# First sequences of attention between two MoE layers: direct rows loaded ahead of q rows, f projected between a group's last two tiles, -|f| ahead of the norm, and a narrower wait for the first scores

## The reference

```
x = x + 0.5 * moe(norm(x))
x = x + attention(norm(x))
x = x + 0.5 * moe(norm(x))
```

## Time and profile before

| what | value |
|---|---|
| median of 3 runs | 469.72 us (466.66 to 469.98) |
| the profiled execution, its own time | 468.03 us |
| its span in the trace | 465.9 us |
| mean granted clock of TensorE | 0.978 |
| busy: PE / DVE / ACT / POOL | 404.1 us (87%) / 362.4 (78%) / 278.5 (60%) / 249.7 (54%) |

### The profile page before, as it was taken

How to read it: one execution, slowest core, us unless ns; L and a number is a source line. 1 busy time by engine, 2 the same in 40 slices (tenths; PEclk the granted TensorE clock), 3 DMA queues, 4 the chain that set the end, 5 groups by cost and what they waited for, 6 DMA issues and landing times.

```text
span 465.9 us, 11688 instructions
## 1 busy us (share of the span) xinstructions
PE 404.1 (87%) x3280; PEld 287.6 (62%) x3296; DVE 362.4 (78%) x1284; ACT 278.5 (60%) x758; POOL 249.7 (54%) x431
## 2 busy tenths in 40 slices
PE   0778888775799999999999999999998898888884
PEld 0656666553466666666667666766765676666652
DVE  3989999986877786686677678677666458999995
ACT  4666777352275566657566566655656567667753
POOL 8976666543245544544554454454445435676654
PEclk9999999887999999999999999999999899999998
DMA  3311000035644354344535535443540000001001
GB/s 112 92 56 22 0 1 0 1 100 148 171 118 152 117 155 116 111 139 111 149 102 147 134 102 149 113 147 108 152 130 9 6 1 1 25 24 45 23 23 45
DMA packets 45792, 39.11 MB, mean 84 GB/s; under 512 B 5896, under 2 KB 42524, under 8 KB 45754
## 3 DMA queue, kind: packets, MB, share of 16 engines
q1 hardware_dynamic: 43706, 38.14, 29.0%
q10 hardware_dynamic: 2048, 0.53, 0.6%
HBM read 22.61 MB, written 15.20 MB: 81 GB/s over the span
## 4 chain that ended last, share of the span: by engine, by line
PE 43%; POOL 22%; issue 14%; ACT 8%; DVE 5%; DMA 2%; ACTq 2%; SPq 2%; POOLq 1%; DVEq 0%
PE bank L916 10%; POOL m_pair L217 9%; PE bank L901 8%; PE bank L886 6%; ACT a_weights L733 5%; POOL m_upper L221 4%; PE bank L889 4%; PE bank L881 4%; POOL m_rstd L229 3%; PE bank L997 2%; PE bank L1008 2%; ACTq L725 2%; PE bank L1011 2%; DVE a_neg_max L794 1%; DMA x_all<-in_L_attn_x 1%
## 5 line engine op out<-in xcount | busy, mean ns | idle before, releaser
L794 DVE TENSOR_REDUCE a_neg_max<-bank 128x2 f32<-128x512 f32 (+1 forms) x192 | 123.7, 685 | 62.6 <-PE bank L889 59.9
L673 POOL TENSOR_SCALAR_AFFINE_SELECT a_weights<-a_weights 128x512 f32<-128x512 f32 (+1 forms) x96 | 75.5, 787 | 108.7 <-ACT a_weights L733 104.0
L733 ACT ACTIVATE a_weights<-bank 128x512 f32<-128x512 f32 x192 | 107.0, 591 | 35.0 <-issue 22.0
L251 ACT ACTIVATE m_scaled<-bank,m_gates 128x128 f32<-128x128 f32 x256 | 72.3, 365 | 26.2 <-PE bank L417 26.2
L901 PE MATMUL bank<-a_q_rows,a_k_rows 106*128 106x512 f32 (+1 forms) x192 | 73.7, 451 | 4.9 <-ACT a_weights L733 4.9
L217 POOL TENSOR_TENSOR m_pair<-m_scaled 128x256 f32<-128x256 f32 x64 | 47.5, 742 | 50.8 <-ACT m_scaled L251 50.7
L294 DVE SCALAR_TENSOR_TENSOR m_lower<-bank,m_gates,m_lower 128x128 f32<-128x128 f32 x192 | 66.0, 344 | 2.3 <-issue 0.2
L886 PE MATMUL bank<-a_k_rows,a_q_rows 104*128 104x256 f32 x256 | 59.3, 335 | 0.4 <-DVE a_neg_max L794 0.4
L889 PE MATMUL bank<-a_mask,a_ident 128*128 128x256 bf16 (+1 forms) x176 | 56.2, 320 | 0.0
L916 PE MATMUL bank<-a_weights,a_v 128*32 128x128 f32 x1536 | 52.7, 279 | 0.0
L886 PEld LDWEIGHTS bank<-a_k_rows,a_q_rows 104*128 104x128 f32 x256 | 40.6, 194 | 14.5 <-DVE a_neg_max L794 10.1
(11 more groups left out here) (128 smaller groups left out, 828.5 us busy)
## 6 DMA issues: line engine op xcount, KB each, us to landing
a_k_rows<-k_stage SPq DMA_DIRECT2D x16, 416.0 KB
k_stage<-a_k_parts SPq DMA_DIRECT2D x48, 128.0 KB, 1.8
q_stage<-a_q_parts SPq DMA_DIRECT2D x48, 128.0 KB, 1.9
a_q_rows<-q_stage SPq DMA_DIRECT2D x64, 96.0 KB
a_k_heads<-k_stage SPq DMA_DIRECT2D x64, 52.0 KB
a_q_dense<-q_stage SPq DMA_DIRECT2D x16, 192.0 KB
x_all<-in_L_attn_x SPq DMA_DIRECT2D x8, 256.0 KB, 2.8
out_x<-x_all SPq DMA_DIRECT2D x8, 256.0 KB, 2.3
```

The lines of the kernel that those rows point to most:

```text
L251: last = nc.scalar.activation(scaled[:, q % 2, j], y_high[q % 2][:, j * D:(j + 1) * D], ACT.Copy, scale=gates[:, s % 2, q, 4 + j:5 + j])
L673: nc.gpsimd.affine_select(out=diagonal, in_=diagonal, compare_op=ALU.is_ge, fill=0.0, base=0, pattern=[[0, heads.stop - heads.start], [1, P]],
L733: nc.scalar.activation(weights[n // 2][:, half:half + 4, :].rearrange("p h n -> p (h n)"), wt_bank[n % 2][:, :], ACT.Exp).then_inc(wt_exp, 1)
L794: nc.vector.tensor_reduce(neg_max[:, t, heads], score_bank[p % 2][:, :].rearrange("p (h n) -> p h n", n=(t + 1) * P), AX.X, ALU.max, negat ...
```

## The change

Five edits. (1) The string for both early steps becomes `amamamamaa`: attention's part 3 (statistics of s + 3, f on PE) stands between the MoE's tiles 2 and 3 instead of after both. (2) ACT copies f out in part f_part(s) and no longer one part later when s < 0. (3) On DVE -|f| is written ahead of xn; this changes the order only where both fall into the same part, j = 4, for s < 0. (4) SP, for s = -1, loads the direct rows first, then q rows and k rows; for s >= 0 the order stays. In both cases the k_heads loads are now preceded by waits for the stores of k and c. (5) PE's first scores wait until DVE's m_lower chain has 4 x 31 links done and ACT has scaled 31 tiles, instead of for all 32 tiles finished and scaled. The waits for rows_in and direct_in stay.

```diff
--- before.py
+++ after.py
@@ -60,8 +60,8 @@
                 moe(i_moe, i_moe, done)
 
     moe_steps(moe1, -2, groups - 2, after)
-    beside("amamammaaa", -2, moe1, groups - 2)
-    beside("amamammaaa", -1, moe1, groups - 1)
+    beside("amamamamaa", -2, moe1, groups - 2)
+    beside("amamamamaa", -1, moe1, groups - 1)
     run_steps(eng, lambda i, s: [attention(i, s, k) for k in range(6)], 0, seqs - 1, (2, 2 + (seqs - 5) // 3 * 3), 3)
     beside("amaamamaam", seqs - 1, moe2, -2)
     beside("amaamamaam", seqs, moe2, -1)
@@ -460,7 +460,7 @@
         return part
 
     return dict(load_group=load_group, store=store, gpsimd=gpsimd, scalar=scalar, vector=vector, tensor=tensor,
-                tiles_done=upper_used, high_used=high_used)
+                tiles_done=upper_used, high_used=high_used, low_chain=low_chain)
 
 
 def attention_layer(nc, ctx, c, made, banks, x_all, S_LEN, before):
@@ -589,6 +589,18 @@
                     wait_apart(sp, scores_ready, i * 12 + 1, sp_waited)
                 at_least(sp, wt_ready, (i - 1) * 12)
                 sp.wait_ge(q_stored, n * 16 * 3)
+
+                def load_direct():
+                    sp.dma_start(raw(q_dense)[0:NG * 3 * HD, :, :],
+                                 q_dram[b, :, :, :, 0:P].rearrange("r g u n -> (r g) u n")).then_inc(direct_in, 16)
+                    sp.wait_ge(k_stored, n * 16 * 3)
+                    sp.wait_ge(c_stored, n * 16 * 2)
+                    for g in range(NG):
+                        sp.dma_start(raw(k_heads)[g:KR:NG, NU * g:NU * (g + 1), :],
+                                     k_dram[b, :, g, :, 0:P]).then_inc(direct_in, 16)
+
+                if s < 0:
+                    load_direct()
                 for g in range(NG):
                     sp.dma_start(raw(q_rows[b])[g:NG * 3 * HD:NG, NU * g:NU * (g + 1), :],
                                  q_dram[b, :, g]).then_inc(rows_in, 16)
@@ -597,11 +609,7 @@
                 sp.dma_start(raw(k_rows[b])[0:KR, :, :], k_dram[b].rearrange("r g u n -> (r g) u n")).then_inc(rows_in, 16)
                 if 0 <= s:
                     sp.wait_ge(scores_ready, i * 12 + 4)
-                sp.dma_start(raw(q_dense)[0:NG * 3 * HD, :, :],
-                             q_dram[b, :, :, :, 0:P].rearrange("r g u n -> (r g) u n")).then_inc(direct_in, 16)
-                for g in range(NG):
-                    sp.dma_start(raw(k_heads)[g:KR:NG, NU * g:NU * (g + 1), :],
-                                 k_dram[b, :, g, :, 0:P]).then_inc(direct_in, 16)
+                    load_direct()
             if 0 <= s + 2 < NSEQ:
                 b, n = (s + 2) % 3, i + 3
                 sp.wait_ge(qk_lo_done, n * 2)
@@ -750,7 +758,7 @@
                                      ACT.Copy).then_inc(v_copied, 1)
             if j == 3 and S:
                 copy_max(i, s, 0)
-            if j == f_part(s) + 1 and F:
+            if j == f_part(s) + (1 if s >= 0 else 0) and F:
                 act.wait_ge(f_ready, n)
                 nc.scalar.activation(f[:, :], proj_bank[0:H, 0:N], ACT.Copy).then_inc(f_copied, 1)
             if j == f_part(s) + 2 and F:
@@ -840,13 +848,13 @@
                 if s <= 0:
                     dve.wait_ge(before["tiles_done"], 2 * (s + 4) if s < 0 else 2 * NSEQ)
                 statistics(i + 3, n + 1)
-            if j == 4 and 0 <= s + 3 < NSEQ:
-                wait_apart(dve, xt_ready, n, dve_waited)
-                normalised(i + 3, n + 1)
             if j == f_part(s) + 1 and F:
                 dve.wait_ge(f_copied, n)
                 nc.vector.scalar_tensor_tensor(out=neg_abs[:, :], in0=f[:, :], scalar=-1.0, in1=f[:, :],
                                                op0=ALU.mult, op1=ALU.min).then_inc(neg_abs_done, 1)
+            if j == 4 and 0 <= s + 3 < NSEQ:
+                wait_apart(dve, xt_ready, n, dve_waited)
+                normalised(i + 3, n + 1)
             if j == 3 and T:
                 normalise(i - 2, s - 2, 1)
             if j == f_part(s) + 2 and F:
@@ -938,8 +946,8 @@
             if s == 0 and j == 0:
                 pe.wait_ge(set_up, 2)
                 pe.wait_ge(ones_in, 16 * 3 * (NG + 3))
-                pe.wait_ge(before["tiles_done"], 2 * NSEQ)
-                pe.wait_ge(before["high_used"], 2 * NSEQ)
+                pe.wait_ge(before["low_chain"], 4 * (2 * NSEQ - 1))
+                pe.wait_ge(before["high_used"], 2 * NSEQ - 1)
 
             if j == 0 and S:
                 pe.wait_ge(rows_in, (i + 1) * 16 * LOADS)
```

## The result

| | median us (lowest to highest), 12 runs each | ratio to before (95%) |
|---|---|---|
| before, beside it | 466.97 (465.03 to 469.98) | |
| after, first set | 470.44 (467.30 to 473.02) | 1.0064 (1.0035 to 1.0092) |
| after, second set, another session | 467.76 (465.27 to 472.53), before 467.22 | 1.0003 (0.9969 to 1.0038) |

The first set is slower by 0.64%, beyond its interval. The second set of the same kernel shows nothing. Both sets together have a mean of 469.19 us (24 runs); before, over the three sessions of the experiments, has 467.77 (104 runs): the change costs some 1.4 us (0.4 to 2.4 by the spread of the runs), under the 1% that I had called measurable, and of the other sign than my -0.12. One execution of before and one of e12, both of 2020 us, are left out of every mean and ratio here. The profiled execution took 470.74 us (span 468.6) where before took 468.03 (465.9).

A forecast was written before the change was run, and what follows sets the result against it. The attention loop was taken as PE-bound (15.98 of 16.59 us), the first score as waiting on DVE's low parts, SP's issues and the last load. Reorder +0.70 and schedule -0.82 gave -0.12: median 469.72 becomes 469.6 us, range 466.0 to 472.0.

The forecast's parts named there:

- my -0.12: First score at the seam before attention: net shift forecast, +0.70 for the reorder less 0.82 for the schedule, in us.
- The reorder, +0.70: Sequence 0's loads: k rows (416 KB) become last, landing 3.55 us after issue, so the first score comes 0.70 us later.
- the one built on the q rows tile: Upper bound for the k rows' landing: 4.4 us for 96 KB plus 1.2 for the rest, 5.6 us; +3.3 in all.
- late k rows: Rival at the last load: k rows queue behind q rows, land 5.5 us after issue; +1.8, so 471.5 us; chance 0.17.
- The schedule, -0.82: DVE before sequence 0's xn: the wait for rstd disappears, low parts done 0.82 us sooner; ends 0.4 and 1.4.
- The waits, 0: PE's first scores: the relaxed wait, met 4.1 us early and hidden by the loads, is worth 0.
- The clock rival: PE's first scores, 111.2 to 117.6 us: less time at 1.2 GHz, -1.6, so 468.0 us; chance 0.13.
- marks set in advance: Signs expected in the profile after: low parts, load order, last issue, first score and releaser, sequence 1's stores and score, loop pace.

The follow-up runs named there:

- e12: Before with only the narrower wait of the first scores: 469.04 us, ratio 1.0019 (0.9982 to 1.0056).
- e2: Before with only the schedule edits (f between the last two tiles, earlier copy of f, -|f| ahead of the norm): 466.37 us, ratio 0.9998.
- e3: After with the old load order put back, so schedule edits and narrower wait: 465.28 us, ratio 0.9955 to before.
- e11: e3 with -|f| moved back behind the norm: 466.16 us, ratio 0.9965 to before.
- e1: Before with only the new load order for the first sequence (direct rows first, then q rows and k rows): 468.78 us, ratio 1.0031.
- e4: After unchanged, the second set with a second profile: 467.76 us, ratio 1.0003 to before.
- e7: After, with SP waiting for sequence 0's rows to land before issuing sequence 1's stores: 467.87 us, ratio 1.0013 to before.
- e9: After with 16 matmuls whose output nobody reads, in PE's idle time ahead of the first score: 466.12 us, ratio 0.9955 to before.
- e6: After with q rows loaded behind k rows for the first sequence, so a q rows load is last: 466.79 us, ratio 0.9978 to before.
- e5: After, with sequence 0's first scores awaiting only the direct rows, and the other rows two parts later: 466.19 us, ratio 0.999 to before.
- e10: e3 with 10 matmuls whose output nobody reads in the idle time ahead of the first score: 465.03 us, ratio 0.9943 to before.

## Why the prediction was wrong

**The reorder, +0.70: this term was mis-sized, and most of all by its landing.** From the first load issue to the first score the old order takes 9.53 to 10.44 us (before, e12, e2, e3, e11: 10.44, 10.21, 9.81, 9.53, 10.29; mean 10.1), the new one 11.60 to 13.06 (after, e1, e4, e7, e9: 12.31, 11.77, 13.06, 11.84, 11.60; mean 12.1). It costs **2.1 us** (12.12 less 10.06). I drew a line between whole loads of 256 and 512 KB and took 3.55; the k rows landed in 4.15 to 4.70. Those rows are of the inputs, loaded at the start of the kernel; the k rows are gathered from the stage and go behind nine other loads. Which of these differences makes them later no run separates. Of the bounds, the one built on the q rows tile pointed to the right side, and it was put aside for a row "nearest in size". The other half of the error is on the side removed: the last k heads load was taken at its one row of 3.31, and landed in 2.40 to 3.31, 2.93 in the mean of five. The issue times were right: the last issue 7.37 us behind the first (8.20 in e4, by its late c rows), forecast 7.35 and 0.1 for c, where before had 6.99. So the 2.1 is 0.4 of issue (with 0.1 of waiting for c in it; e4 waited 0.8 more), 4.43 (mean of four) less 2.93 = 1.5 of landing, and 0.1 that PE starts 0.24 and not 0.14 us behind it.

**The rival "late k rows"** had this mechanism, deciding from 3.7 us, at a chance of 0.17. My reason against it, that no queue builds up, did not keep the k rows from landing late: 4.15 us even with the stores 2.6 us behind. Whether a queue did build up is not shown. Its size for the landing, 5.5, was too large. I had noted that sequence 1's stores start sooner and priced their meeting with the k rows at nothing: it is 0 to 0.4 us.

**The schedule, -0.82: the mechanism was right.** The 0.82 us of waiting is gone in every profile with the new schedule. The low parts are done there at 94.2 to 96.0, and at 95.07 to 96.56 in the three without; much of this scatter lies ahead of all edits, in when DVE makes sequence 0's xn (84.19 to 85.97). Counted from there they take 10.0 to 10.6 us in ten of the eleven profiles with the new schedule (11.0 in e6), and 10.8, 10.8 and 11.85 without. e1 and e2, with the granted clock at 1.00 there, differ by 0.7; before and e3, at 0.79, by 1.3. So 0.7 to 1.3, within the bounds 0.4 to 1.4. That the subtraction parts from the GpSimd addition, an end of my range, isn't shown: it takes 0.39 us after and 0.74 before, but 0.25 and 0.27 in e1 and e12 with the old schedule.

**The waits, 0: right.** e12 shows it, and e5 why the relaxed wait and the direct rows can't pay as they stand: the first score awaits the rows as well. That this was the limit is only half true, though; without it the next limit is DVE's order, and a third of the gain remains.

**The clock rival came in part, and was taken back.** I gave 0.13 to a shorter stretch at the low level, while naming in its disfavour that PE's idle time in front grows. It did, from 4.4 to 7.95 and 8.82 us, because both halves add to it: the tiles finish sooner and the loads land later. Even so the first step got shorter, from 14.09 to 13.23 and 13.51 us (1.6 were forecast by the rival), and from 111 to 118 us the granted clock was 0.53 before and 0.70 after (0.56 in e4). But a second low stretch followed, 0.72 over 125 to 131 us in both profiles of after where before had 1.00. From the first score to sequence 3's it takes 46.30 and 45.61 us after, 45.60 before: the clock there costs 0 to 0.7 us. The length of the idle time does not order these: e4 with 8.82 us has 45.61, e1 with 5.81 has 46.17, e3 with 5.30 has 45.64.

What e9 says of it: it keeps the new load order and fills the idle time, and the mean falls to 466.17 at a mean clock of 0.9857. That filling it pays in the kernel after is what the runs show; that the idle time is what the change lost by is not shown, and how the 3.0 us divide is not either. In the profiles, e9's first score came 0.92 us later than after's and its sequence 3 0.27 us sooner (156.91 against 157.18, and 157.67 in e4), so the first seam gives 0.3 to 0.8 us in absolute time. But e9's profile was already 1.6 to 1.7 us late at sequence 0's xn, ahead of all edits. Counted from there it gains 1.9 us against after and 2.5 against e4: 0.7 and 2.0 before the first score, where its loads came sooner, which the matmuls don't explain, and 1.2 and 0.5 between the first score and sequence 3's, which can be the clock. In e10 against e3 that last stretch is 0.3 us longer. Another 3.6 us lie at the second seam against the one profile of after, and nothing (30.06 against 30.05) against e4. Why idle time at 103 us should bear on a seam at 350 no run here shows, and it may not.

**What of the 1.4 us is accounted for.** Reorder +2.1 and schedule -0.7 to -1.3 leave +0.8 to +1.4 at the first score. Counted from sequence 0's xn, the first score comes after 26.54 and 27.83 us in the two profiles of after (26.12 in e7, 25.83 in e9) and after 26.50 and 25.23 in those of before and e12, +0.7 in the means. At sequence 3's first score +0.4 (after) and +0.9 (e4) are there in absolute time, against before's 156.81. So about half of the 1.4 or more is what the mis-sized load leaves, and the rest is of the size of the clock's changes at both seams. The fit at equal clock would put all of it down to the clock, but the same fit has e1 1.1 us above before and e3 2.2 below after, which is the order's cost again; the fit can't separate a stall from the clock in it and behind it. The share of each stays open.

The median of the first set, 470.44, lies inside the range of 466.0 to 472.0, and even within 1 us of 469.6. That is luck: the three runs of before that I started from have a median of 469.72, 2.75 us above that of its twelve; beside those the change stands at +3.5 in this set and +0.5 in the second, and not at -0.12. Of the marks set in advance, the new order, the release by k rows, sequence 1's first score some 14 us behind the first (13.23) released by DVE, and the pace (16.5) came true; the last issue at 105.94 came 1.5 us sooner than the 107.4 named, the first score at 110.88 close to 111.1, by two errors that cancel: low parts 1.3 us sooner than the 95.7 named, and a landing 1.15 us later than 3.55. Sequence 1's stores came at 106.44 and not at 108.5: they follow the last load issue at once, as I had said, but I had not moved them by my own -0.82, and that issue was sooner still.

## What to carry to other kernels

Where a consumer waits for a count of all loads, only the last one matters: price a reordering by the landing of the transfer that becomes last, taken from loads issued in the same burst, and by what is released to follow it on the same queue. Work that ends sooner in front of a load that does not only lengthens TensorE's idle time; what the clock then takes was 0 to 0.7 us here, and the length of the idle time did not foretell it. And when a kernel's own runs spread by 5 us, compare the mean granted clock beside the time, look in which stretches it differs and whether the engine had work there, and repeat a set before believing 0.6%.

## What the runs showed of the hardware

- The last load of this burst of ten landed later than loads of more bytes at the start of the kernel: 416 KB in 4.15 to 4.70 us, where 512 KB took 4.0. 96 KB as the last took 3.29 (e6). A 52 KB last load varied by 0.9 us between profiles (2.40 to 3.31).
- With 7 us of matmuls that compute nothing of use, in front of a stage that the load held back anyway, the mean of after fell by 3.0 us; in e3, with 5.3 us of idle time, such matmuls changed nothing that can be told. In the profile after, PE idles for 7.95 us; the granted clock is 0.50, the level of 1.2 GHz, from 106 us until 114, three us into the first scores (the 0.68 over 111.2 to 117.6 is a mean of both levels). In e9, without the idle time, the first scores have 1.00. The Trainium skill, "TensorE: Matmul & The Clock Gate", section "HAM oscillation — how this bites in real kernels", describes such a burst behind a wait for a DMA that starts at the slow level. The trace agrees, with 0.50 from the first score at 110.88 to 114.
- The granted clock late in a run differs between executions of one kernel: after had 0.86 in one and 1.00 in another (e4) over 350 to 386 us, and the second seam took 33.7 and 30.05 us, a difference of 3.6, more than the change under study.
